# Pair interactions and MLP tower: a ScalarE copy ahead of every second product, reordered front loads, and another unit dissolved

## The reference

```python
e = stack([tbl_f[ids[:, f]] for f in range(40)], axis=1)      # 512 x 40 x 32
z = einsum('bpd,pde,bpe->bp', e[:, iidx], bilinear, e[:, jidx])  # 780 pairs
h = concatenate([z, dense_ctx], axis=1)                       # 512 x 796
h = maximum(h @ W_top1 + b_top1, 0)                           # 512 wide
h = maximum(h @ W_top2 + b_top2, 0)                           # 256 wide
y = h @ W_top3
```

## Time and profile before

| what | value |
|---|---|
| median of 3 runs | 176.49 us (175.66 to 176.54) |
| the profiled execution, its own time | 176.31 us |
| its span, first to last instruction | 174.5 us |
| granted TensorE clock, mean over the span | 1.000 |
| PE busy, share of the span | 168.0 us, 96% |
| DVE | 145.4 us, 83% |
| ACT | 43.6 us, 25% |
| POOL | 115.1 us, 66% |

### The profile page before, as it was taken

One profiled execution on the slowest core, in us unless ns is written; L12 is line 12 of the kernel. 1 busy time (PEld: TensorE's weight loads), 2 busy tenths in 40 slices (PEclk: granted clock), 3 DMA queues, 4 the chain that ended last, 5 costly groups with the idle time before them and its releaser, 6 DMA issues.

```text
span 174.5 us, 4015 instructions
## 1 busy us (share of the span) xinstructions
PE 168.0 (96%) x1710; PEld 53.5 (31%) x1710; DVE 145.4 (83%) x144; ACT 43.6 (25%) x58; POOL 115.1 (66%) x119
## 2 busy tenths in 40 slices
PE   6899999999899999999999999999999999999993
PEld 2234444332232323233223232332323323232220
DVE  1799998896699999899999899999999999993600
ACT  2489993220011210012110021112001121100503
POOL 3777777777777777777777777777899982122000
PEclk9999999999999999999999999999999999999999
DMA  5999987997414711010105640001000660000000
GB/s 144 370 422 398 418 244 212 318 325 215 148 43 122 229 24 18 12 15 15 15 11 128 175 105 15 15 11 19 11 2 19 165 180 4 2 0 4 0 0 0
DMA packets 12698, 19.95 MB, mean 114 GB/s; under 512 B 3828, under 2 KB 6776, under 8 KB 12552
## 3 DMA queue, kind: packets, MB, share of 16 engines
q1 hardware_dynamic: 9144, 18.03, 31.0%
q0 software_dynamic: 3072, 1.58, 5.5%
q10 hardware_dynamic: 464, 0.09, 0.3%
HBM read 11.82 MB, written 0.00 MB: 68 GB/s over the span
## 4 chain that ended last, share of the span: by engine, by line
PE 88%; DVE 4%; ACT 3%; DMA 2%; issue 1%; SPq 0%; DVEq 0%
PE y_ps L551 33%; PE z_ps L622 26%; PE t_ps L522 10%; PE y_ps L565 8%; PE y_ps L522 7%; DVE prod L505 3%; PE t_ps L565 2%; DMA hot_id<-hot_ids 2%; PE z_ps L565 1%; DVE hot L482 1%; ACT plane L408 1%; ACT xt L427 0%; ACT hot_id L465 0%; ACT xt L428 0%; PE t_ps L643 0%
## 5 line engine op out<-in xcount | busy, mean ns | idle before, releaser
L505 DVE TENSOR_TENSOR prod<-y_ps,xt 128x1024 f32<-128x1024 f32 x98 | 114.8, 1219 | 10.8 <-DMA xt<-xt 3.8
L336 POOL DMA_INDIRECT x_rows<-rows,row x96 | 92.1, 959 | 29.2 <-issue 29.0
L551 PE MATMUL y_ps<-xt,m_sb 32*128 32x512 f32 x392 | 61.6, 640 | 0.5 <-issue 0.5
L622 PE MATMUL z_ps<-prod,sel 128*32 128x512 f32 x392 | 52.2, 604 | 0.6 <-issue 0.4
L522 PE MATMUL t_ps<-z_t,table 128*32 128x256 f32 x352 | 27.1, 379 | 0.0
L482 DVE TENSOR_SCALAR hot<-hot_id,number 128x2048 bf16<-128x2048 int16 x34 | 22.9, 751 | 4.1 <-DMA hot_id<-hot_ids 4.1
L551 PEld LDWEIGHTS y_ps<-xt,m_sb 32*128 32x128 f32 x392 | 18.4, 182 | 24.7 <-DVE prod L505 13.7
L522 PEld LDWEIGHTS t_ps<-z_t,table 128*32 128x32 f32 x352 | 11.4, 110 | 26.4 <-issue 26.4
L622 PEld LDWEIGHTS z_ps<-prod,sel 128*32 128x32 f32 x392 | 7.8, 107 | 37.4 <-DVE prod L505 20.1
L565 PE MATMUL y_ps<-hot,plane 128*32 128x512 bf16 x200 | 15.1, 379 | 0.2 <-ACT plane L408 0.2
L344 POOL TENSOR_TENSOR hot_id<-x_rows,hot_id 128x512 f32<-128x512 f32 x6 | 7.6, 1274 | 11.6 <-ACT x_rows L451 11.6
(11 more groups left out here) (39 smaller groups left out, 62.2 us busy)
## 6 DMA issues: line engine op xcount, KB each, us to landing
xt<-xt SPq DMA_DIRECT2D x18, 192.0 KB, 2.5
xt<-xt SPq DMA_DIRECT2D x17, 128.0 KB, 2.4
hot_id<-hot_ids SPq DMA_DIRECT2D x4, 512.0 KB, 6.0
xt<-xt SPq DMA_DIRECT2D x32, 64.0 KB, 2.0
x_rows<-rows,row POOLq DMA_INDIRECT x96, 2.3
table<-hot_tables SPq DMA_DIRECT2D x2, 640.0 KB, 8.4
table<-w SPq DMA_DIRECT2D x1, 1280.0 KB, 6.6
table<-hot_tables SPq DMA_DIRECT2D x2, 512.0 KB, 5.2
```

The source lines that it names most:

```text
L336: pool.indirect_dma_start(out=x_rows[:, g, c, :], out_offset=None, in_=rows, in_offset=bass.IndirectOffsetOnAxis(ap=row[:, n:n + 1], axis= ...
L505: nc.vector.tensor_tensor(prod[:, k % PROD_UNITS, 2 * half:2 * half + 2, :], y_ps[:, 2 * slot:2 * slot + 2, :], partners[half], ALU.mult). ...
L551: last = nc.tensor.matmul(y_ps[:, 2 * slot + place(t, u, s) % 2, :], m_sb[rows, k, :], xt[rows, moving(t, u, s), :], start=True, stop=True)
L622: last = nc.tensor.matmul(z_ps[s * DIM:(s + 1) * DIM, :], window, prod[:, k % PROD_UNITS, place(*UNIT[k], s), :], start=first, stop=(k == ...
```

## The change

Four edits:

- **ScalarE copies** the second half of each unit from unit 2 on (`COPY_FROM`) from `y_ps` to `y_copy`, a ring of two in the last third of the storage of `hot`, which is free by then. The copy of unit k stands ahead of everything else of step k in ScalarE's order. Pk.1 takes both of its inputs from SBUF and waits for `y_copied` in place of `y_done`. Y's half n whose half n-3 is a second half waits for that copy and no more for the product.
- **The front's DMAs**: SP issues only the first four chunks of matrices (12 units) at the start, w1's first blocks after the mixes of groups 0 and 1 as before, then the mixes of groups 2 and 3, and only then the other five chunks, the rest of w1 and w2. w2 has a semaphore of its own.
- **Another unit dissolved**: `SPLIT` is (5, 0) in place of (3, 0). Unit (3, 0) comes back as number 4, the old numbers 4 to 6 become 5 to 7 ((3, 1), (2, 2), (3, 3)), (4, 0) to (4, 3) become 8 to 11, (5, 0) is gone, and from number 12 on the list is the same. The diagonal units of even t now read x5 where they read x3.
- **Turns and the early unit**: group 2 is turned ahead of unit 1 in place of unit 2, group 4 ahead of unit 8 in place of 7, and the first steps of unit 1 stand ahead of round 34 in place of 35.

```diff
--- before.py
+++ after.py
@@ -20,7 +20,7 @@
 G = P // DIM
 GROUPS = FIELDS // G
 COUPLES = GROUPS // 2
-SPLIT = (3, 0)
+SPLIT = (5, 0)
 UNITS = GROUPS * GROUPS // 2 - 1
 PER_BLOCK = DIM // G
 BLOCKS = -(-UNITS // PER_BLOCK)
@@ -121,12 +121,16 @@
 
 
 HEAD_AFTER = 2
+REST_AFTER = 4
+MATS_EARLY = 4
 W1_EARLY = 5
 
 
 Y_SLOTS = 3
 PROD_UNITS = 4
 LAG = 2
+COPY_RING = 2
+COPY_FROM = 2
 
 
 WARM = 14
@@ -136,7 +140,7 @@
 BY_SCALAR = {14: 0, 33: 1}
 ONES_RING = 2
 
-EARLY_UNIT = {31: 0, 35: 1}
+EARLY_UNIT = {31: 0, 34: 1}
 PIECE_RING = 2
 HOT_BANK = [(0, 1), (2, 3), (4, 5), (6, 7)]
 
@@ -160,7 +164,7 @@
 
 AFTER = {
     "l1": list(range(5, UNITS)),
-    "turn": [2, 7, 17, 23, 31, 39],
+    "turn": [1, 8, 17, 23, 31, 39],
 }
 
 
@@ -254,6 +258,8 @@
         w1_sb = weight_cols[:, 0:BLOCKS * N1].rearrange("p (b n) -> p b n", b=BLOCKS)
 
         hot_cols = hot[:].rearrange("p n f c -> p (n f c)").bitcast(F32)
+        y_copy = hot_cols[:, 2 * M1 * BATCH:2 * M1 * BATCH + COPY_RING * 2 * BATCH].rearrange(
+            "p (n h b) -> p n h b", n=COPY_RING, h=2)
         plane_cols = plane[:].rearrange("p n s f c -> p (n s f c)").bitcast(F32)
         row_cols = x_rows[:].rearrange("p g c d -> p (g c d)")
         part_sb = [None, hot_cols[:, 0:M1 * BATCH], hot_cols[:, M1 * BATCH:2 * M1 * BATCH], plane_cols[:, 0:M1 * BATCH],
@@ -298,6 +304,7 @@
         w1_in = sem("w1_in")
         w1_rest_in = sem("w1_rest_in")
         head_in = sem("head_in")
+        w2_in = sem("w2_in")
         gathered = [sem(f"gathered{g}") for g in range(GATHERS)]
         mats_in = [sem(f"mats_in{c}") for c in range(len(MAT_CHUNKS))]
         plane_done = [sem(f"plane_done{o}") for o in range(HOTS)]
@@ -311,6 +318,7 @@
         t_out = sem("t_out")
         y_done = sem("y_done")
         prod_done = sem("prod_done")
+        y_copied = sem("y_copied")
         sum_done = sem("sum_done")
         z_out = sem("z_out")
         dense_there = sem("dense_there")
@@ -365,7 +373,7 @@
             load_tables(2)
             load_hot_ids(3)
             load_tables(3)
-            for c in range(len(MAT_CHUNKS)):
+            for c in range(MATS_EARLY):
                 load_mats(c)
             sp.dma_start(b1_sb[:], b1).then_inc(head_in, 16)
             sp.dma_start(b2_sb[:], b2).then_inc(head_in, 16)
@@ -374,9 +382,12 @@
             for g in range(GROUPS):
                 if g == HEAD_AFTER:
                     sp.dma_start(w1_sb[:, 0:W1_EARLY, :], w1[:, 0:W1_EARLY, :]).then_inc(w1_in, 16)
+                if g == REST_AFTER:
+                    for c in range(MATS_EARLY, len(MAT_CHUNKS)):
+                        load_mats(c)
                     sp.wait_ge(hot_used, len(ROUND))
                     sp.dma_start(w1_sb[:, W1_EARLY:, :], w1[:, W1_EARLY:, :]).then_inc(w1_rest_in, 16)
-                    sp.dma_start(w2_sb[:], w2).then_inc(head_in, 16)
+                    sp.dma_start(w2_sb[:], w2).then_inc(w2_in, 16)
                 if g >= 2 * MIX_RING:
 
                     sp.wait_ge(prod_done, 2 * UNIT.index((g - 2 * MIX_RING, g - 2 * MIX_RING)) + 2)
@@ -426,6 +437,15 @@
                 act.wait_ge(hot_used, picked(o))
                 nc.scalar.activation(halves(words, BF16)[:, :, 1], hot_bank(o, 0), ACT.Copy).then_inc(x_out, 1)
                 nc.scalar.activation(halves(words, U16)[:, :, 0], hot_bank(o, 1), ACT.Copy).then_inc(x_out, 1)
+
+            def copy_half(k):
+
+                slot = (2 * k + 1) % Y_SLOTS
+                act.wait_ge(y_done, 2 * k + 2)
+                if k >= COPY_FROM + COPY_RING:
+                    act.wait_ge(prod_done, 2 * (k - COPY_RING) + 2)
+                nc.scalar.activation(y_copy[:, k % COPY_RING, :, :], y_ps[:, 2 * slot:2 * slot + 2, :],
+                                     ACT.Copy).then_inc(y_copied, 1)
 
             make_planes(0)
             make_planes(1)
@@ -438,12 +458,14 @@
             rebuild(2)
             rebuild(3)
             for what, k in steps:
+                if what == "unit" and k >= COPY_FROM:
+                    copy_half(k)
                 if what == "l1" and k % 2 == 1:
                     b, m = L1_STEP[k // 2]
                     act.wait_ge(part_done, k // 2 + 1)
                     if b == 0:
                         if m == 0:
-                            act.wait_ge(head_in, 16 * 4)
+                            act.wait_ge(head_in, 16 * 3)
                         nc.scalar.activation(h1[:, m, :], t_ps[:], ACT.Identity, bias=b1_sb[:, m:m + 1]).then_inc(t_out, 1)
                     else:
                         if m == 0 and part_free[b]:
@@ -492,18 +514,25 @@
                 if u == t:
                     dve.wait_ge(mixed[t], 16 * len(mix_pieces(t)))
                     x_there(dve, t ^ 1)
+                    if t % 2 == 0 and t > 0:
+                        x_there(dve, SPLIT[0])
                     pairs = [sorted(partner(t, u, s) for s in (2 * half, 2 * half + 1)) for half in range(2)]
                     partners = [xt[:, low:high + 1:high - low, :] for low, high in pairs]
                 else:
                     partners = [xt[:, t, :].unsqueeze(1).to_broadcast([P, 2, BATCH])] * 2
                 for half in range(2):
                     slot = (2 * k + half) % Y_SLOTS
-                    dve.wait_ge(y_done, 2 * k + half + 1)
+                    if half == 0 or k < COPY_FROM:
+                        dve.wait_ge(y_done, 2 * k + half + 1)
+                        first_step = y_ps[:, 2 * slot:2 * slot + 2, :]
+                    else:
+                        dve.wait_ge(y_copied, k - COPY_FROM + 1)
+                        first_step = y_copy[:, k % COPY_RING, :, :]
                     if half == 0 and k >= PROD_UNITS:
 
                         dve.wait_ge(sum_done, k - PROD_UNITS + 1)
                     nc.vector.tensor_tensor(prod[:, k % PROD_UNITS, 2 * half:2 * half + 2, :],
-                                            y_ps[:, 2 * slot:2 * slot + 2, :], partners[half],
+                                            first_step, partners[half],
                                             ALU.mult).then_inc(prod_done, 1)
             dve.wait_ge(sum_done, UNITS)
             nc.vector.tensor_copy(z_t[:, BLOCKS - 1, :], z_ps[:]).then_inc(z_last, 1)
@@ -543,8 +572,11 @@
                     half = 2 * k + s // 2
                     slot = half % Y_SLOTS
                     if s % 2 == 0 and half >= Y_SLOTS:
-
-                        pe.wait_ge(prod_done, half - Y_SLOTS + 1)
+                        k_before, half_before = divmod(half - Y_SLOTS, 2)
+                        if half_before == 0 or k_before < COPY_FROM:
+                            pe.wait_ge(prod_done, half - Y_SLOTS + 1)
+                        else:
+                            pe.wait_ge(y_copied, k_before - COPY_FROM + 1)
                     elif s % 2 == 0:
                         pe.wait_ge(x_out, 2 * half + 2)
                     rows = slice(s * DIM, (s + 1) * DIM)
@@ -628,6 +660,7 @@
                 pe.wait_ge(prod_done, LATE_READ[m])
                 by_columns(y_ps[:, LATE_BANK[m], :], w1_sb[:, BLOCKS - 1, m * P:(m + 1) * P],
                            z_t[:, BLOCKS - 1, :], m not in LATE_PARTS, True).then_inc(l1_done, 1)
+            pe.wait_ge(w2_in, 16)
             for m in range(M1):
                 pe.wait_ge(l1_out, m + 1)
                 for c in range(M2):
```

## The result

The changed kernel takes 179.95 us (median of six runs, 179.74 to 195.03) against 176.51 before in the same series: ratio 1.020, 95% interval 1.017 to 1.023. **It is slower by 2%**, where 174.9 and a range of 173.2 to 177.4 were forecast. The span of the profiled execution is 178.2 us, 3.7 more than before.

A forecast was written before the change was run, and what follows sets the result against it. TensorE was taken to bound the steady part at 2.50 us a unit. The front gains 2.05 less 0.50 for x4's turn: 176.31 − 1.55 = 174.76, with the median 0.18 higher, 174.9 us; range 173.2 to 177.4.

The forecast's parts named there:

- What bounds the kernel: Steady part: TensorE bounds it at 2.50 us a unit; VectorE has 0.23 us to spare a unit.
- the freed slots: Steady part: the copy frees second-half slots that TensorE never waited for; gain 0, also at transposes.
- ScalarE's copy: Each unit from 2 on: 1.02 us for 1024 columns, bounds 0.9 and 1.19; fits with nothing to spare.
- P3.1 behind the `dense` issues: Front: copy 3 waits for ScalarE's `dense` issues, so P3.1 starts at 39.93 where 38.69 was possible; costs 1.24 us.
- The two waits for mixes: Front: the diagonal units' products P5 and P6 stop waiting for mixed tiles; both waits, 3.0 us, go.
- The product from SBUF: VectorE's second-half product with two SBUF inputs: 1.13 us, unchanged; upper bound 1.48, which would cost 5 us.
- rival A: Beside GpSimd's joins, two-SBUF-input products and joins wait for each other: 177.4 us, or 181.9 if GpSimd always leads; 0.20 with D.
- D: Each two-input product stops a GpSimd gather and every turn is late: over 185 us; left small, within rival A.
- GpSimd's gathers: If the new product slows them for half the time, 75 gathers come 3 us late, just hidden.
- Late loads: The remaining 3.4 MB start near 41 us; unit 12, first to need them, is due near 60: cost 0.

The follow-up runs named there:

- join_write_only: The changed kernel with GpSimd's 18 joins replaced by memsets that write SBUF without reading it: 175.97 us, ratio 0.995 to the kernel before.
- copy_to_38: The changed kernel with ScalarE's copies for units 2 to 37 only, none beside the joins: 175.95 us, ratio 0.995 to the kernel before.
- no_copy: The changed kernel without ScalarE's copies, every product from PSUM, all other edits kept: 173.98 us, ratio 0.987 to the kernel before.
- copy_only: The kernel before with ScalarE's copies and the waits on them alone, nothing else of the change: 179.88 us, ratio 1.019 to the kernel before.

## Why the prediction was wrong, point by point

- **What bounds the kernel: right.** 2.50 us a unit on TensorE, 71.64 and 71.66 us from Y10 to Y38 with and without copies. That the freed slots give nothing held too.
- **ScalarE's copy: right.** 1025 ns on the page, forecast 1020, and it fits between the products.
- **P3.1 behind the `dense` issues: right**, 40.06 for 39.93; Y6 44.96 for 44.89. The two waits for mixes went as forecast.
- **The product from SBUF: the step that failed.** "I take 1.13, unchanged." With no join that reads beside it it is so: 1217 ns mean in join_write_only. Beside the joins it is 2.30 in every second unit. The mechanism stood in the text as rival A, at 0.20 with D, for want of a row; copy_to_38 and join_write_only show that it costs 4.0 us. The rule of the Trainium skill that was named there, SBUF — State Buffer (Who interferes with whom), is what the trace shows: the later one is blocked until the other's end, by joins of 1.27 us that read and not by memsets that only write. Nothing in the trace of before spoke against it: the earlier trace rows are of a stretch in which no VectorE instruction had two SBUF inputs, and a rule about exactly this pair should have had the greater chance.
- **A's price was too low as well.** 1.5 us for the products and 1.0 for the end were set; 3.33 and 0.62 were measured; the time lies between A's two prices, 177.4 and 181.9. The step was "VectorE loses one or two such waits". In fact three joins fit into the 5.72 us of two units, and six products waited: those of units 38 and 39 (2.17 and 1.65 us; Y40 to Y41 takes 3.92 in place of 2.95 and the next step 2.70 in place of 2.50), and 41, 43, 45 and 47 (2.29 or 2.30), three of which cost TensorE 0.72 each by Y48: 0.97 + 0.20 + 3 × 0.72 = 3.33.
- **GpSimd's gathers: mis-sized.** I allowed 3 us in all by a slowing of 8% in the hot phase; 3.9 us were lost behind 28 us, in holds of up to 1 us. The size was near, but the two largest holds (36.60 and 42.44, 1.83 us together) fell among the gathers of x4, the one group without slack.
- **Late loads: mis-sized.** "0" was right for unit 12, which was asked, and not for the gathers beside them. x4 landed at 47.2 before, 49.7 with the new loads (no_copy), 48.9 with the copies (copy_only), 52.1 with both; due at 51.2. The holds and the late landing together make 1.0 of the 1.24 us between forecast and measurement at Y10. The other 0.2 was there before: Y7 came 0.07 late, and the step to Y8 took 2.63 in place of 2.50.

Of the 5.21 us between the forecast span and the measured one, 3.95 are thus the joins, 1.04 the gather of x4 and 0.20 the steps up to Y8.

## What to carry to other kernels

Before an operand of a VectorE instruction is moved from PSUM to SBUF, look at what GpSimd reads in the same microseconds: here two SBUF inputs made the two engines take turns, and TensorE, which bounds the kernel, paid 3.95 us for it. A copy that relieves a buffer is worth nothing where that buffer was not what the bound engine waited for; the start times show that ahead of any experiment. When a load is moved off one transfer's path, name the transfer that it will lie beside next, the indirect ones above all.

## What the hardware showed that was not expected

- One GpSimd copy after another (0.56 us each, one SBUF input) kept a waiting product out for twelve of them; it took 7.41 and 7.37 us in the two traces; joins (two inputs, 1.27 us) let it in after one. Why they differ is open.
- The order of two starts 0.04 to 0.05 us apart decides which engine loses 1.1 us.
- An indirect DMA's issue on GpSimd is held by a product with two SBUF inputs that already runs: it ends 0.82 us behind the product, so that 0.94 becomes up to 1.93. One that starts in the product's last 0.12 us loses nothing.
- A transpose of 128 columns takes 302 ns, one of 512 takes 702, so four pieces cost 0.5 us more busy time than the whole.
